# Casts of weights re-spread around a first attention, and a reordered start with zero products, in a three-part layer on eight cores

## What is computed

```python
x = batch[b]                                            # [2048, 1024] float32, one per core
x = x + 0.5 * ffn(layernorm(x))                         # int32 weights, scaled by 1/127
x = x + attention_and_mlp(layernorm(x))                 # float32 weights
x = x + 0.5 * ffn(layernorm(x))

def ffn(x):        return (silu(x @ Wg.T) * (x @ Wu.T)) @ Wd.T      # 1024 -> 3072 -> 1024
def attention_and_mlp(x):
    q, k, v = heads(x @ Wq), heads(x @ Wk), heads(x @ Wv)  # 16 heads of 64
    qp, kp = phi(q), phi(k)                # 128 features: exp(proj - max) / sqrt(128) + 1e-6
    a = causal_linear_attention(qp, kp, v) # running sums of kp v and kp over the rows
    h = layernorm(x + a @ Wo, eps=1e6)
    return relu(h @ W1 + b1) @ W2 + b2                      # 1024 -> 4096 -> 1024
```

## Time and profile before

| | us |
|---|---|
| median of 3 runs (lowest, highest) | 1813.14 (1812.77, 1820.92) |
| the profiled execution | 1805.6 |
| its span on core 4, the slowest | 1804.0 |
| spans of the eight cores | 1782.2 to 1804.0 |
| TensorE busy with products | 1752.6 (97%) |
| DVE, ACT, Pool busy | 774.6, 442.9, 186.6 |

### The profile page before, as it was taken

How to read it: one execution, slowest core, us unless ns; L and a number is a source line. 1 busy time by engine, 2 the same in 40 slices (tenths; PEclk the granted TensorE clock), 3 DMA queues, 4 the chain that set the end, 5 groups by cost and what they waited for, 6 DMA issues and landing times.

```text
span 1804.0 us, 29674 instructions; the slowest of 8 cores (1782.2 to 1804.0 us)
## 1 busy us (share of the span) xinstructions
PE 1752.6 (97%) x9232; PEld 832.5 (46%) x9232; DVE 774.6 (43%) x1697; ACT 442.9 (25%) x982; POOL 186.6 (10%) x354
## 2 busy tenths in 40 slices
PE   5999999999998899999999999999999999999999
PEld 2444444444554344444444444444444444444444
DVE  5453115511785244666465433567533110431341
ACT  2221002202553125422332430233241130010110
POOL 3111101100021130103000000300001110000000
PEclk9999999999999999999999999999999999999999
DMA  9998957999999965787556775746666564544543
GB/s 201 238 224 170 190 152 153 188 217 204 238 180 170 191 201 153 171 185 189 167 149 177 186 208 179 198 141 175 173 192 192 170 178 153 171 158 154 199 152 105
DMA packets 198901, 324.54 MB, mean 180 GB/s; under 512 B 125792, under 2 KB 125920, under 8 KB 198752
## 3 DMA queue, kind: packets, MB, share of 16 engines
q1 hardware_dynamic: 185936, 277.49, 55.0%
q0 software_dynamic: 12240, 44.11, 17.1%
q10 hardware_dynamic: 576, 1.05, 0.2%
HBM read 311.12 MB, written 52.43 MB: 202 GB/s over the span
## 4 chain that ended last, share of the span: by engine, by line
PE 92%; DMA 5%; SPq 1%; DVE 1%; issue 1%; ACT 1%; DVEq 0%; POOL 0%; ACTq 0%; POOLq 0%
PE d_ps L876 35%; PE d_ps L916 31%; PE d_ps L893 17%; DMA fmZ<-aotm 3%; PE a_ps L989 2%; PE d_ps L989 2%; DMA x_tm<-xin 2%; SPq L322 1%; PE a_ps L450 1%; PE a_ps L548 1%; PE a_ps L451 1%; ACT ftm L471 0%; DMA ring<-gu_i 0%; PE a_ps L574 0%; PE a_ps L502 0%
## 5 line engine op out<-in xcount | busy, mean ns | idle before, releaser
L916 PE MATMUL d_ps<-ring,big 128*128 128x512 bf16 x2176 | 488.1, 380 | 0.1
L916 PEld LDWEIGHTS d_ps<-ring,big 128*128 128x128 bf16 x2176 | 207.5, 98 | 233.6 <-issue 1.9
L876 PE MATMUL d_ps<-fmX,ring 128*128 128x512 bf16 x1152 | 267.6, 383 | 1.2 <-ACT fmX L347 1.2
L1053 ACT ACTIVATE th_t<-d_ps 128x512 f32<-128x512 f32 x192 | 115.0, 599 | 617.8 <-PE d_ps L876 616.2
L876 PE MATMUL d_ps<-fmZ,ring 128*128 128x512 bf16 x1152 | 255.7, 379 | 0.1
L1164 DVE SCALAR_TENSOR_TENSOR th_t<-th_t,d_ps 128x512 f32<-128x512 f32 x192 | 131.6, 685 | 210.0 <-ACT th_t L1053 209.5
L471 ACT ACTIVATE ftm<-a_ps,nmax 128x128 bf16<-128x128 f32 x512 | 146.3, 369 | 242.4 <-DVE nmax L458 238.2
L876 PE MATMUL d_ps<-fmY,ring 128*128 128x512 bf16 x768 | 169.5, 379 | 1.4 <-ACT fmY L347 1.4
L876 PEld LDWEIGHTS d_ps<-fmZ,ring 128*128 128x128 bf16 x1152 | 110.6, 98 | 126.2 <-issue 0.2
L876 PEld LDWEIGHTS d_ps<-fmX,ring 128*128 128x128 bf16 x1152 | 109.9, 99 | 122.4 <-issue 6.2
L893 PE MATMUL d_ps<-fmX,ring 128*128 128x512 bf16 x640 | 143.5, 379 | 0.0
(11 more groups left out here) (80 smaller groups left out, 1376.8 us busy)
## 6 DMA issues: line engine op xcount, KB each, us to landing
ring<-gu_b SPq DMA_DIRECT2D x144, 512.0 KB, 4.1
ring<-w_b SPq DMA_DIRECT2D x128, 512.0 KB, 3.9
ring<-d_b SPq DMA_DIRECT2D x72, 512.0 KB, 4.4
w_b<-w_f POOLq DMA_DIRECT2D x32, 512.0 KB, 12.5
ring<-gu_i POOLq DMA_DIRECT2D x24, 512.0 KB, 11.5
gu_b<-ring SPq DMA_DIRECT2D x24, 512.0 KB, 17.7
ring<-q_b SPq DMA_DIRECT2D x16, 512.0 KB, 10.4
ring<-k_b SPq DMA_DIRECT2D x16, 512.0 KB, 9.3
```

The lines of the kernel that those rows point to most:

```text
L876: r = e.matmul(d_ps[bank][:, :], ring[:, so + g * 1024 + k * 128:so + g * 1024 + (k + 1) * 128], xT[:, k * 512:(k + 1) * 512], start=(k == ...
L916: r = e.matmul(d_ps[t][:, :], lhs[:, o:o + 128], ring[:, so + i * 512:so + (i + 1) * 512], start=(s == 0 and i == 0), stop=(s == n_slots - ...
L1053: e.activation(th_t[:, (n % 2) * 512:(n % 2 + 1) * 512], d_ps[2 * (n % 2)][:, :], AF.Tanh, scale=TANH_SC).then_inc(s_tanh, 1)
```

## The change

Eight edits, in two places of the program.

In the start: (1) DVE clears a tile `zero` first, and TensorE multiplies it by itself, 30 products before the first transpose and 3 after each of the first three. (2) `ident` is loaded before x tiles 2 and 3 and has its own semaphore `s_id`; TensorE and ACT no longer wait for the other constants at the start. (3) Slot 0 is loaded once x tile 0 is in, slot 2 ahead of the statistics of block 1, slot 3 behind x tile 6, slots 4 to 7 behind the `rstd` of x tile 7. (4) The transform of x tile 1 runs on ACT (`lntm` = `rstd` * x + `nmr`, `nmr` from Pool), and the DVE takes the statistics of tiles 2 and 3 before it transforms tile 2. (5) The first pair of products is made of products of 256 columns, the first half of which needs only tiles 0 and 1 evicted. (6) The ticks of block 1 start two ticks later and follow at every tick instead of every second (2, 1, 1 for 0, 2, 2).

In the casts: (7) the 48 pieces are issued at other places.

| pieces issued | before | after |
|---|---|---|
| with the int32 slots | 6 | 6 |
| in the second half of the first down products | 0 | 6 |
| gate/up of block 2 | 12 | 10 |
| down of block 2 | 4 | 4 |
| q, k of block 0 | 3 | 5 |
| in the first attention | 22 | 11 |
| right behind it | 1 | 0 |
| at wo(0), one every 4 of 16 product groups | 0 | 4 |
| behind the `rstd` of the sum of block 0 | 0 | 2 |

(8) `s_cw2` is split in two, for the first and the last 8 pieces of w2.

```diff
@@ dve_ln_xform
-                            ALU.subtract, ALU.mult).then_inc(s_lxf, 1)
+                            ALU.subtract, ALU.mult).then_inc(s_lxf, 2 if m == 2 else 1)
@@ pe_ln_transpose
-            e.wait_ge(s_lxf, m + 1)
+            if m == 1:
+                e.wait_ge(s_axf, 1)
+            else:
+                e.wait_ge(s_lxf, m + 1)
@@ pool_attn
-                if b == 0 and s % 7 in (1, 4):
+                if b == 0 and s % 7 == 1:
                     cast_piece(e)
@@ sp_program
-            for t in range(4):
+            for t in range(2):
                 e.dma_start(xt(t)[:, 0:512],
                             xin[t * 128:(t + 1) * 128, 0:512]).then_inc(s_x[t], 16)
-            e.dma_start(ident[:, :], idb_in).then_inc(s_const, 16)
+            e.dma_start(ident[:, :], idb_in).then_inc(s_id, 16)
+            for t in range(2, 4):
+                e.dma_start(xt(t)[:, 0:512],
+                            xin[t * 128:(t + 1) * 128, 0:512]).then_inc(s_x[t], 16)
...
-                    e.wait_ge(s_cw2, 256)
+                    e.wait_ge(s_cw2[0], 128)
+                if n == SL_GU2 + 24 + 12 + 12 + 36 + 16 + 16 + 8:
+                    e.wait_ge(s_cw2[1], 128)
@@ pool_program
-            e.wait_ge(s_x[1], 32)
+
+            e.wait_ge(s_x[0], 32)
             e.dma_start(slot(0), slots[0][0], max_dma_last_dim=8192).then_inc(s_lc[0], 16)
             e.wait_ge(s_half, 1)
             pool_ln_rstd(e, LN1, 0, 0)
             pool_ln_rstd(e, LN1, 0, 1)
+            n1 = st_no(LN1, 0) + 1
+            e.wait_ge(s_rstd, n1 + 1)
+            e.tensor_scalar(nmr[:, 0:1], mv[:, 2 * n1:2 * n1 + 1], rstd[:, n1:n1 + 1], -1.0,
+                            ALU.mult, ALU.mult).then_inc(s_nmr, 1)
             e.dma_start(slot(1), slots[1][0], max_dma_last_dim=8192).then_inc(s_lc[1], 16)
             pool_ln_rstd(e, LN1, 0, 2)
             pool_ln_rstd(e, LN1, 0, 3)
-            for n in range(2, RING):
+            e.dma_start(slot(2), slots[2][0], max_dma_last_dim=8192).then_inc(s_lc[2], 16)
+            pool_ln_rstd(e, LN1, 1, 0)
+            pool_ln_rstd(e, LN1, 1, 1)
+            e.wait_ge(s_x[6], 16)
+            e.dma_start(slot(3), slots[3][0], max_dma_last_dim=8192).then_inc(s_lc[3], 16)
+            pool_ln_rstd(e, LN1, 1, 2)
+            pool_ln_rstd(e, LN1, 1, 3)
+            for n in range(4, RING):
                 e.dma_start(slot(n), slots[n][0], max_dma_last_dim=8192).then_inc(s_lc[n], 16)
             e.dma_start(omT[:, :], omD_in).then_inc(s_om, 16)
-            for j in range(4):
-                pool_ln_rstd(e, LN1, 1, j)
...
+            for i in range(6, 12):
+
+                e.wait_ge(s_d, 8 * i)
+                cast_piece(e)
             for i in range(N_GU):
...
-                if i % 2 == 0:
+                if i % 12 in (1, 3, 5, 8, 10):
                     e.wait_ge(s_up, 48 + i)
                     cast_piece(e)
             for i in range(4):
                 e.wait_ge(s_d, 96 + 12 * i + 4)
                 cast_piece(e)
-            for i in range(3):
-                e.wait_ge(s_qk, 5 * i + 1)
+            for i in range(5):
+                e.wait_ge(s_qk, 3 * i + 1)
                 cast_piece(e)
             for b in range(NB):
                 pool_attn(e, b)
                 if b == 0:
-                    for i in range(3):
+
+                    for i in range(N_O):
+                        e.wait_ge(s_wo, 4 * i + 1)
                         cast_piece(e)
...
                 for j in range(4):
                     pool_rstd(e, sti_no(b) + j, 1e6)
+                if b == 0:
+                    cast_piece(e)
+                    cast_piece(e)
@@ pe_program
+            def first_pair(so):
+
+                st["pair"] += 1
+                for half in range(2):
+                    e.wait_ge(s_lev, 2 * half + 2)
+                    for g in range(2):
+                        for k in range(8):
+                            o = k * 512 + half * 256
+                            r = e.matmul(d_ps[g][:, half * 256:(half + 1) * 256],
+                                         ring[:, so + g * 1024 + k * 128:
+                                              so + g * 1024 + (k + 1) * 128],
+                                         fmX[:, o:o + 256], start=(k == 0), stop=(k == 7))
+                        if half:
+                            r.then_inc((s_gate, s_up)[g], 1)
+                for g in range(2):
+                    freed[g] = ((s_gm, 1), (s_h, 1))[g]
...
-            e.wait_ge(s_const, 64)
+
+            def busy(n):
+                for i in range(n):
+                    e.matmul(d_ps[3][:, :], zero[:, 0:128], zero[:, :], start=True, stop=True)
+
+            e.wait_ge(s_zero, 1)
+            busy(30)
+            e.wait_ge(s_id, 16)
             for j in range(4):
                 pe_ln_transpose(e, LN1, 0, j, j)
+                if j < 3:
+                    busy(3)
 
             def first(k):
-                pe_ln_tick(e, LN1, 1, k, 0, 2)
+                pe_ln_tick(e, LN1, 1, k, 2, 1, 1)
                 pe_ln_tick(e, LN1, 2, k, 24, 6, 5)
...
-                pair(held[i], (fmX, fmY)[bb], side)
+                if (bb, i) == (0, 0):
+                    first_pair(held[i])
+                    side()
+                    side()
+                else:
+                    pair(held[i], (fmX, fmY)[bb], side)
@@ act_program
-            e.wait_ge(s_const, 64)
+            n1 = st_no(LN1, 0) + 1
+            e.wait_ge(s_nmr, 1)
+            e.activation(lntm[:, 1024:2048], xt(1), AF.Identity, bias=nmr[:, 0:1],
+                         scale=rstd[:, n1:n1 + 1]).then_inc(s_axf, 1)
             for j in range(4):
                 act_ln_evict(e, LN1, 0, j, j)
+            e.wait_ge(s_const, 48)
@@ dve_program
-            for j in range(4):
-                dve_ln_stats(e, LN1, 0, j)
-                if j > 0:
-                    dve_ln_xform(e, LN1, 0, j - 1)
+            e.memset(zero[:, :], 0.0).then_inc(s_zero, 1)
+            dve_ln_stats(e, LN1, 0, 0)
+            dve_ln_stats(e, LN1, 0, 1)
+            dve_ln_xform(e, LN1, 0, 0)
+            dve_ln_stats(e, LN1, 0, 2)
+            dve_ln_stats(e, LN1, 0, 3)
+            dve_ln_xform(e, LN1, 0, 2)
             dve_ln_xform(e, LN1, 0, 3)
```

More of the change, by code:

```diff
@@ L102, in build @@
         warm = sbuf("warm", 1, F32)
+        zero = sbuf("zero", 512, BF16)
+        nmr = sbuf("nmr", 1, F32)
         bst = sbuf("bst", 24, F32)
@@ L120, in build @@
         s_x = [sem(f"s_x{t}") for t in range(16)]
-        s_const = sem("s_const")
+        s_const, s_id = sem("s_const"), sem("s_id")
         s_b2r = sem("s_b2r")
@@ L126, in build @@
         s_half = sem("s_half")
+        s_zero, s_nmr = sem("s_zero"), sem("s_nmr")
         s_lc = [sem(f"s_lc{j}") for j in range(RING)]
@@ L130, in build @@
         s_cq, s_ck, s_cv, s_co = sem("s_cq"), sem("s_ck"), sem("s_cv"), sem("s_co")
-        s_cw1, s_cw2 = sem("s_cw1"), sem("s_cw2")
+        s_cw1, s_cw2 = sem("s_cw1"), (sem("s_cw2a"), sem("s_cw2b"))
         s_out = sem("s_out")
         s_bst, s_mv, s_veps, s_rstd = sem("s_bst"), sem("s_mv"), sem("s_veps"), sem("s_rstd")
-        s_lxf, s_ltr, s_lev = sem("s_lxf"), sem("s_ltr"), sem("s_lev")
+        s_lxf, s_axf, s_ltr, s_lev = sem("s_lxf"), sem("s_axf"), sem("s_ltr"), sem("s_lev")
         s_xb = (sem("s_xb0"), sem("s_xb1"))
@@ L781, in build @@
                   + [(w1_b, w1_f, i, s_cw1) for i in range(N_W1)]
-                  + [(w2_b, w2_f, i, s_cw2) for i in range(N_W2)])
+                  + [(w2_b, w2_f, i, s_cw2[i // 8]) for i in range(N_W2)])
         n_cast = [0]
@@ L1096, in act_program @@
             e.activation(warm[:, :], phalf[:, :], AF.Tanh).then_inc(s_warm, 1)
-            e.wait_ge(s_const, 64)
+            n1 = st_no(LN1, 0) + 1
+            e.wait_ge(s_nmr, 1)
+            e.activation(lntm[:, 1024:2048], xt(1), AF.Identity, bias=nmr[:, 0:1],
+                         scale=rstd[:, n1:n1 + 1]).then_inc(s_axf, 1)
             for j in range(4):
                 act_ln_evict(e, LN1, 0, j, j)
+            e.wait_ge(s_const, 48)
             def first(k):
-                act_ln_tick(e, LN1, 1, k, 0, 2)
+                act_ln_tick(e, LN1, 1, k, 2, 1, 1)
                 act_ln_tick(e, LN1, 2, k, 24, 6, 5)
@@ L1234, in attn @@
                 return spread(lambda bb, s: dve_attn(e, bb, s), b, ticks)
-            for j in range(4):
-                dve_ln_stats(e, LN1, 0, j)
-                if j > 0:
-                    dve_ln_xform(e, LN1, 0, j - 1)
+            e.memset(zero[:, :], 0.0).then_inc(s_zero, 1)
[5 more added lines that the diff above has]
+            dve_ln_xform(e, LN1, 0, 2)
             dve_ln_xform(e, LN1, 0, 3)
             def first(k):
-                dve_ln_tick(e, LN1, 1, k, 0, 2)
+                dve_ln_tick(e, LN1, 1, k, 2, 1, 1)
                 dve_ln_tick(e, LN1, 2, k, 24, 6, 5)
```

2 lines of the change are left out of this document (removed).

## The result

The changed kernel takes 1808.44 us (median of 16 runs, 1805.32 upward), the kernel before 1820.75 in the same session (11 runs, 1812.77 upward). The ratio is 0.9938, 95% interval [0.9922, 0.9953]: faster by 0.6%, where 1785 against 1813.14, or 0.9845, was forecast, with a range of 1774 to 1801. The profiled execution took 1808.77. That of before took 1805.6, less than any timed run of its kernel, so profile against profile shows +3 us and runs against runs about -11. That its stalls vary from run to run, and that its profile holds a mild case, is my reading; it has one profile only.

A forecast was written before the change was run, and what follows sets the result against it. Two stretches were taken as gapless TensorE, leaving DMA-caused losses in head and first attention. Core 4: 1804.0 - 7.3 - 18.5 = 1778.2; slowest core 1780, profiled 1782, plus half the 7.5 us median gap: 1785 us, range 1774 to 1801.

The forecast's parts named there:

- The attention stall: First attention: with thinned casts the DMA queue stops growing; the stretch takes 205 us, 21 below core 4.
- the two waits: First attention, core 4: 7.33 us before an item's output product and 12.47 us before wo(0), both from late aotm transposes.
- Rivals 1 and 3: 1: transposes beside any cast stay slow, 1796, chance 0.14. 3: casts aren't the cause, only the head gains, 1808, 0.07.
- The wait at w1(0): End of first attention: moved casts delay the fmX transposes; 2.5 us of TensorE wait taken, between none and 15.8.
- rival 2: The wait moves to w1(0), transposes at the 22.9 us median: 15.8 us instead of 2.5, total 1798, chance 0.10.
- The head: Start up to block 1's first product: 42 us on the slowest core, gaining 7.3 us on core 4, 1 on core 0.
- Slot 4 in at about 37.5: Head: slots 4 to 7 issued at 31 behind tile 7's statistics, slot 4 landing at 37.5, block 1 starting at 41.
- the order changes, not the amount: Head: DMA engines, full from 4 us on, set the pace; the edits only reorder the same loads.
- behind it slots 5 to 7 ... covered: After block 1 starts: these slots are needed every 6.9 us and take 3.7 us each, so no wait.
- the unchanged 402.5: Stretch from block 1's first product to the first attention: TensorE without a gap, 402.5 us before and after.
- signs of being wrong: aotm transposes still over 15 us, block 1 starting after 46, or cores still differing by over 10 us.
- The rule weighed: DMA engines serve queues round-robin, so the casts' queue length wouldn't matter; by it 1796; given a chance, not the sum.

The follow-up runs named there:

- e3_late: Kernel before with the cast edits alone, the last six cast pieces moved into the second attention: 1788.01 us, ratio 0.9848.
- e11_late_again: The kernel before with the cast edits alone and the last six pieces in the second attention, measured again in another session: 1791.86 us, ratio 0.9905.
- e2_head: Changed kernel with the casts put back where they were before, so the head's edits alone: 1818.43 us, ratio 1.0012.
- e6_late_hold: Old head, cast edits with the last six pieces in the second attention, plus only the holding back of slots: 1797.90 us, ratio 0.9890.
- e10_rstd_pieces: Kernel before with the cast edits, the four wo(0) pieces moved to the second attention, the pair behind the rstd left: 1801.50 us, ratio 0.9955.

## Why the prediction was wrong, step by step

**The attention stall: right.** "The queue doesn't grow", and the two waits would go. The transposes landed after 3.4 and 5.4 us, under the 11 named. The stretch needs 201.0 us by measurement (e3_late, e11_late_again), 202.7 from the start that the prediction used, 1.73 us earlier; I had worked out 203 and taken 205. From before's 224.34 on core 4 that is 23 us, 21 forecast. Rivals 1 and 3 are out: 15 pieces in the attention and around it leave no stall, and with the casts put back it returns (e2_head).

**The wait at w1(0): the right term, mis-sized by 7 to 12 us.** The step that failed is "I take 2.5, nearer the first, since the four pieces at wo(0) have mostly drained". The term's own upper end, 15.8 from the 22.9 median, was near the truth: 13.56 on core 4, 9.9 to 14.8 on all. The four had not drained: alone they cost 6.0 to 7.6 us. And without them the wait was still 8.9 to 16.2. I had priced the pair behind the `rstd` by nothing of its own, though Pool issues it in the microseconds in which SP issues the transposes, and SP's queue goes in order: the issue of the first two took 19.29 us, so the last two couldn't even begin. The pair also slows the DVE's last transform to 10.5 us, a path that the sum didn't have. This is rival 2, 1798, to which I gave 0.10; that rival kept the head's gain, and the head fell 15.6 us short on core 4.

**The head: wrong in sign on the typical core.** The zero products from 1.9 us on and the first product at 17 to 18.5 came as forecast, 2 us earlier. Two steps failed. "Slot 4 in at about 37.5": it was in at 43.79 on core 4. I had Pool issue slots 4 to 7 at 31, and it was 36.95: the two `rstd` pairs ahead wait for statistics, and the DVE, which gets x tile 5 only at 27.80 and is busy for 4.72 of 5 us in 30 to 35, reaches these only between its transforms and the products' evictions; I had counted them as if they came straight behind the tile. And "the order changes, not the amount" assumed full DMA engines throughout; an issue held back that long lets them stand, at 0.32 and 0.42 for 10 us. Then "behind it slots 5 to 7 ... covered" and the unchanged 402.5: these looked at the next three slots, not at the whole row up to 140 us, in which the DMA engines are at a share near 1 (0.95 before in 120 to 150), so a loss is hard to make up. It came due as 10.2 us on core 4: 4.5 of wait for slots, twice 1.7 for the products behind them that ran at the lower clock (16 in 5.30 us against 3.62), and most of the rest a wait of 1.85 us for a row tile of block 2.

```profile
118.05 0.61 PE L345 MATMUL a_ps<-ident,lntm 128*128 128x128 bf16 x8 [1.85 <-DVE lntm L313]
```

e6_late_hold shows that the holding of slots in edit 3 does it by itself.

**The rest.** The six casts in the first down products cost nothing, as said (50.00 of 50.00 us busy; a DMA share of 0.92, I had 0.8). Half of the 7.5 us between the median and the profile, 3.7, was added, and the profile after is at its median. By the slowest core: 1780 forecast for its span, 1806.9 on core 0. Of the signs of being wrong, two came: block 1 after 46 (on four cores, up to 49.90), and cores that differ by over 10 us (10.9). A slip without weight: of the kernel before I counted 3 pieces behind the attention, and the table of the change has the right 1.

**The rule weighed.** The rows first: the two pieces behind the `rstd` cost a wait of 11.06 us, six 12.25, and a piece that leaves Pool 3 us after SP has issued the last transpose (638.82 against 631.71 + 4.19), none. By the round-robin that the Trainium skill states in "DMA: Bandwidth & Descriptors", "Queues, rings and completion order", it matters whether the other queue holds anything, not how long it is: here the trace agrees, though both waits hold the DVE's slow transform too, and I had given the backlog the weight. At the same rate of casts, 10.7 and 22.9 us before the change remain unexplained by it.

## What to carry to other kernels

When work is moved off a stall, price its new place by the landings of the worst stretch seen, not by those of a mean one, and look there for what is issued in the same microseconds on a queue that goes in order. Before a load is held back behind another engine's result, add up what the DMA engines have left to do until the share falls below 1: here a hole at 30 to 40 us came due as waits at 126 and 137. When a cost has moved once, measure the rest of the kernel too: moved again, a part of it came back in the second attention. And compare stretches of all cores rather than spans, since here the profile of before was faster than every timed run of its kernel.

## What the runs showed that was not expected

- The issue of a DMA transpose is no fixed cost to SP: about 1.3 us each on core 4 of e3_late (median), but up to 13.6 us for one on core 4 of the profile after, beside cast pieces.
- One DVE transform of 128x1024 in float32 took 10.48 us where the other three took 0.8; it starts 0.67 us ahead of Pool's four adds (below) and ends 0.55 us behind them. Before, the longest was 2.6 us, and the same adds took 9.90 us instead of 9.26. The pair of pieces behind the `rstd` separates the two cases on all cores of all profiles. With it Pool's adds begin behind the transform's start, without it 0.4 to 0.5 us ahead of it; that this order is what matters is likely, but no run changes it by itself. It didn't set the time in after, where SP's queue was later by 8 us; in e10_rstd_pieces the queue was later by 2.

```profile
645.51 9.26 POOL L877 TENSOR_TENSOR x_tm<-x_tm,b2r_s 128x1024 f32<-128x1024 f32 x4
```

- The landing of a cast piece was 14.6 us in the median beside the transposes of fmX and 8.2 in the second attention of e3_late, with the issue rate one in 8 us there.
